# Splitting a gate/up stage into two token halves, and where a layer norm and the down weights then stand

## What is computed

```python
x = x + _layernorm(_L0_attn_ref(_layernorm(x), W_spin, b_spin, W_global, W_J, beta))
x = x + _layernorm(_L0_ffn_ref(_layernorm(x), w_gate, w_up, w_down))

# _L0_ffn_ref: D = 1024, H = 3072, int32 weights scaled by 1/127
gate = einsum('bsd,hd->bsh', x, wg); up = einsum('bsd,hd->bsh', x, wu)
h = silu(gate) * up
return einsum('bsh,dh->bsd', h, wd)
```

## Time and profile before

| | us |
|---|---|
| median of 2 runs (1460.48 to 1469.74) | 1465.11 |
| the profiled execution, slowest core | 1465.29 |
| its span in the trace (core 2) | 1463.7 |
| spans of the eight cores | 1441.8 to 1463.7 |
| PE busy in the span | 1208.2 (83%) |
| DVE, ACT, POOL busy | 494.7, 222.4, 72.9 |

### The profile page before, as it was taken

One profiled execution on the slowest core, in us unless ns is written; L12 is line 12 of the kernel. 1 busy time (PEld: TensorE's weight loads), 2 busy tenths in 40 slices (PEclk: granted clock), 3 DMA queues, 4 the chain that ended last, 5 costly groups with the idle time before them and its releaser, 6 DMA issues.

```text
span 1463.7 us, 14919 instructions; the slowest of 8 cores (1441.8 to 1463.7 us)
## 1 busy us (share of the span) xinstructions
PE 1208.2 (83%) x5274; PEld 517.7 (35%) x5274; DVE 494.7 (34%) x860; ACT 222.4 (15%) x359; POOL 72.9 (5%) x92
## 2 busy tenths in 40 slices
PE   0888887788989999999889810179999999999997
PEld 0233332233433434334333300034444444444443
DVE  2243334113434333333334246822122121134343
ACT  0111111211221111112211110021111111100000
POOL 0011110000000000000000000010110111000000
PEclk9999998989999999999989965589999999999999
DMA  9755557461232222122321179963463737323332
GB/s 191 144 138 131 133 131 179 98 101 28 52 65 44 51 44 43 44 51 44 62 52 38 36 151 242 298 100 36 45 75 40 86 32 84 30 62 111 98 104 86
DMA packets 230393, 131.04 MB, mean 90 GB/s; under 512 B 204720, under 2 KB 204720, under 8 KB 230320
## 3 DMA queue, kind: packets, MB, share of 16 engines
q10 hardware_dynamic: 156672, 50.35, 17.2%
q0 software_dynamic: 57744, 29.37, 15.5%
q1 hardware_dynamic: 15904, 50.37, 12.2%
HBM read 92.31 MB, written 25.17 MB: 80 GB/s over the span
## 4 chain that ended last, share of the span: by engine, by line
PE 62%; DVE 11%; DMA 11%; ACT 6%; ACTq 5%; issue 3%; DVEq 0%; SPq 0%
PE ps_pv L710 17%; PE ps_d L1136 11%; PE ps_u L1043 11%; PE ps_g L1032 11%; DMA xnT_sb<-xn_bf 6%; PE ps_s L256 6%; ACT P_sb L592 4%; ACTq L612 4%; DMA x_sc<-x_buf 3%; PE ps_e L305 2%; DVE tmp L728 1%; DVE qm L567 1%; DVE tmp L733 1%; ACT attn_wb L746 1%; PE ps_q L548 1%
## 5 line engine op out<-in xcount | busy, mean ns | idle before, releaser
L710 PE MATMUL ps_pv<-s_tok,PT_sb 128*128 128x512 bf16 x1024 | 249.1, 409 | 52.0 <-DVE PT_sb L673 51.1
L1032 PE MATMUL ps_g<-xn2T,wg_sb 128*128 128x512 bf16 x768 | 176.1, 388 | 100.7 <-DMA xn2T<-xn_bf 100.7
L548 PE MATMUL ps_q<-s_FM,ebuf 128*128 128x512 bf16 x1024 | 226.7, 382 | 7.6 <-DMA ebuf<-e_sc 7.6
L710 PEld LDWEIGHTS ps_pv<-s_tok,PT_sb 128*128 128x128 bf16 x1024 | 105.1, 104 | 195.9 <-issue 93.7
L1043 PE MATMUL ps_u<-xn2T,wu_sb 128*128 128x512 bf16 x768 | 169.7, 379 | 0.0
L1136 PE MATMUL ps_d<-wdT_sb,h_act 128*128 128x512 bf16 x768 | 165.9, 379 | 1.0 <-DVE h_act L1066 1.0
L1066 DVE SCALAR_TENSOR_TENSOR h_act<-silu_b,ps_u 128x512 bf16<-128x512 f32 x96 | 66.0, 688 | 266.5 <-PE ps_u L1043 265.4
L548 PEld LDWEIGHTS ps_q<-s_FM,ebuf 128*128 128x128 bf16 x1024 | 100.5, 98 | 131.1 <-issue 12.7
L1032 PEld LDWEIGHTS ps_g<-xn2T,wg_sb 128*128 128x128 bf16 x768 | 76.2, 100 | 196.7 <-issue 109.9
L256 PE MATMUL ps_s<-wspT_sb,xnT_sb 128*128 128x512 bf16 x512 | 137.6, 417 | 0.0
L1136 PEld LDWEIGHTS ps_d<-wdT_sb,h_act 128*128 128x128 bf16 x768 | 75.1, 98 | 91.9 <-issue 1.5
(11 more groups left out here) (74 smaller groups left out, 496.9 us busy)
## 6 DMA issues: line engine op xcount, KB each, us to landing
xs<-x SPq DMA_DIRECT2D x24, 1024.0 KB, 7.0
x_sc<-x_buf ACTq DMA_DIRECT2D x16, 512.0 KB, 6.7
xs<-x_sc SPq DMA_DIRECT2D x16, 512.0 KB, 4.3
out<-out_b SPq DMA_DIRECT2D x16, 512.0 KB, 5.1
wg_sb<-wgT POOLq DMA_DIRECT2D x24, 256.0 KB, 4.6
wu_sb<-wuT POOLq DMA_DIRECT2D x24, 256.0 KB, 5.4
wdT_sb<-wdT POOLq DMA_DIRECT2D x4, 1536.0 KB, 16.6
e_sc<-e_stage POOLq DMA_DIRECT2D x32, 128.0 KB, 2.4
```

Source lines behind the costliest of these rows:

```text
L548: i = t.matmul(ps_q[:, slot, half * 512:(half + 1) * 512], ebuf[:, qt % 2, j, :], s_FM[:, j, qi * 1024 + half * 512: qi * 1024 + (half + 1 ...
L710: i = t.matmul(ps_pv2[:, nb * 512:(nb + 1) * 512], PT_sb[:, par, cb * P:(cb + 1) * P], s_tok[:, cb, nb * 512:(nb + 1) * 512], start=(cb == ...
L1032: i = t.matmul(ps_g[:, tb, :], wg_sb[:, par, j, :], xn2T[:, j, tb * 512:(tb + 1) * 512], start=(j == 0), stop=(j == KC - 1))
```

## The change

1. **Token halves.** The FFN runs in two phases: phase 0 over `tb` 0 and 1, phase 1 over `tb` 2 and 3, each over all 24 blocks. A step (`ci`, 0 to 47) is one block in one phase and has 32 matmuls: gate of two `tb`, up of two `tb`. The same gate and up weights are loaded in each phase, so there are 48 pairs of loads where there were 24. The load for step ci+2 waits for the up matmuls of step ci.
2. **L2 in two pieces.** Slots 0 to 8 stay ahead of the FFN. Slots 9 to 15 are emitted one behind each of steps 0 to 6, and slot 16 behind step 7, on the same engines' streams.
3. **Down weights.** All four parts are emitted behind the whole FFN, and each waits for the part before it.
4. **Down matmuls.** A tile's 48 matmuls run in four segments of six hidden blocks, with the two output halves taken in turn; in tile 0 segment k waits for part k of the down weights.

The diff, cut to its core:

```diff
-        for t_i in range(NT_OWN + 1):
+        def l2slot(t_i):
             if t_i < NT_OWN:
                 l2_grpA(t_i)
             if t_i >= 1:
                 l2_grpB(t_i - 1)
-        s_flush()
+        for t_i in range(9):
+            l2slot(t_i)
...
-        def ffn_wload(hb):
-            sem = dwP[hb % 2]
-            w_war = rec.get(("up_mm", hb - 2, 3), 0)
+        def ffn_wload(ci):
+            hb = ci % HC
+            sem = dwP[ci % 2]
+            w_war = rec.get(("up_ci", ci - 2), 0)
...
         def wdT_part(i4):
-            def f(gp, i4=i4):
+            def f(gp, i4=i4, w_self=dwF.n):
+                gp.wait_ge(dwF.h, w_self)
...
-        ffn_wload(0)
-        ffn_wload(1)
-        wdT_part(0)
-
-        for hb in range(HC):
-            par = hb % 2
-            for tb in range(4):
+        def ffn_hb(ph, hb, tbs):
+            ci = ph * HC + hb
+            par = ci % 2
+            for tb in tbs:
...
-                    if hb >= 1:
-                        t.wait_ge(ss.h, rec[("silu", hb - 1, tb)])
+                    if wsl:
+                        t.wait_ge(ss.h, wsl)
...
+        ffn_wload(0)
+        ffn_wload(1)
+        for ph, tbs in ((0, (0, 1)), (1, (2, 3))):
+            for hb in range(HC):
+                ci = ph * HC + hb
+                ffn_hb(ph, hb, tbs)
+                if ci + 2 < 2 * HC:
+                    ffn_wload(ci + 2)
+                if ph == 0 and hb < 7:
+                    l2slot(9 + hb)
+                if ph == 0 and hb == 7:
+                    l2slot(16)
...
-            if hb == 6:
-                wdT_part(1)
-            if hb == 12:
-                wdT_part(2)
-            if hb == 18:
-                wdT_part(3)
...
+        for _i4 in range(4):
+            wdT_part(_i4)
...
-                    t.wait_ge(dwF.h, 64)
...
-                for nb in range(2):
-                    for cb in range(HC):
+                for seg in range(4):
+                    if t_i == 0:
+                        t.wait_ge(dwF.h, 16 * (seg + 1))
+                    for cb in range(seg * 6, (seg + 1) * 6):
+                        for nb in range(2):
```

More of the change, by code:

```diff
@@ L967, in build_program, with f @@
         wdT_r = wdT_d.rearrange("(c p) d -> p c d", p=P)
-        def ffn_wload(hb):
-            sem = dwP[hb % 2]
-            par = hb % 2
-            w_war = rec.get(("up_mm", hb - 2, 3), 0)
-            first = (hb <= 1)
-            def f(gp, hb=hb, sem=sem, par=par, w_war=w_war, first=first):
+        last_silu = {}
+        last_hmul_u = {}
+        last_silu_buf = {}
+        l2_done = {}
+        def ffn_wload(ci):
+            hb = ci % HC
+            sem = dwP[ci % 2]
+            w_war = rec.get(("up_ci", ci - 2), 0)
+            first = (ci <= 1)
+            def f(gp, hb=hb, sem=sem, par=ci % 2, w_war=w_war, first=first):
                 if first:
@@ L995, in ffn_wload @@
             sem.n += 32
-            rec[("wload", hb)] = (sem, sem.n)
+            rec[("wload_ci", ci)] = (sem, sem.n)
         def wdT_part(i4):
-            def f(gp, i4=i4):
+            def f(gp, i4=i4, w_self=dwF.n):
+                gp.wait_ge(dwF.h, w_self)
                 if i4 == 0:
@@ L1013, in wdT_part, with ftg @@
             dwF.n += 16
-        ffn_wload(0)
-        ffn_wload(1)
-        wdT_part(0)
-        for hb in range(HC):
-            par = hb % 2
-            for tb in range(4):
[L1022 to L1025, removed]
+        def ffn_hb(ph, hb, tbs):
+            ci = ph * HC + hb
+            par = ci % 2
+            for tb in tbs:
+                def ftg(t, hb=hb, par=par, tb=tb, first=(tb == tbs[0]),
+                        w4=rec[("xtr4", tb)], wl=rec[("wload_ci", ci)],
+                        wsl=last_silu.get(tb, 0)):
+                    if first:
+                        t.wait_ge(wl[0].h, wl[1])
                     if hb == 0:
@@ L1036, in build_program, with ftu @@
                 block.tensor(ftg)
[L1037 to L1041, removed]
+                rec[("g_ci", ci, tb)] = st.n
+            for tb in tbs:
+                def ftu(t, hb=hb, par=par, tb=tb,
+                        wuh=last_hmul_u.get(tb, 0)):
+                    if wuh:
+                        t.wait_ge(sv.h, wuh)
                     for j in range(KC):
@@ L1047, in build_program, with fsl @@
                 block.tensor(ftu)
[L1048 to L1053, removed]
+                rec[("u_ci", ci, tb)] = st.n
+            rec[("up_ci", ci)] = st.n
+            for tb in tbs:
+                def fsl(s, ci=ci, tb=tb, wt=rec[("g_ci", ci, tb)],
+                        prev=last_silu_buf.get(tb % 2, 0)):
                     s.wait_ge(st.h, wt)
@@ L1060, in build_program, with fvh @@
                 ss.n += 1
[L1061 to L1065, removed]
+                rec[("silu_ci", ci, tb)] = ss.n
+                last_silu[tb] = ss.n
+                def fvh(v, hb=hb, tb=tb, ci=ci,
+                        wsl=rec[("silu_ci", ci, tb)],
+                        wut=rec[("u_ci", ci, tb)]):
+                    v.wait_ge(ss.h, wsl)
+                    v.wait_ge(st.h, wut)
                     i = v.scalar_tensor_tensor(
@@ L1071, in build_program @@
                 block.vector(fvh)
-                rec[("hmul", hb, tb)] = sv.n
-            if hb + 2 < HC:
-                ffn_wload(hb + 2)
-            if hb == 6:
-                wdT_part(1)
-            if hb == 12:
-                wdT_part(2)
-            if hb == 18:
-                wdT_part(3)
[L1082 to L1085, removed]
+                rec[("hmul_ci", ci, tb)] = sv.n
+                last_hmul_u[tb] = sv.n
+                last_silu_buf[tb % 2] = sv.n
+        ffn_wload(0)
[10 more added lines that the diff above has]
+                    l2slot(16)
+                    l2_done.update(
+                        sv=rec[("xn2", NT_OWN - 1)],
+                        ss=rec[("sq3", NT_OWN - 1)],
+                        dt0=dtm[0].n, dt1=dtm[1].n,
+                        da0=da[0].n, da1=da[1].n,
+                        tr=[(s_, s_.n) for s_ in (dtp[0], dtp[1])])
+        hmul_done = rec[("hmul_ci", 2 * HC - 1, 3)]
+        ffn_done = dict(st=rec[("up_ci", 2 * HC - 1)],
+                        ss=rec[("silu_ci", 2 * HC - 1, 3)], sv=hmul_done)
+        ctx2.close()
         ctx23.close()
         ctxPS.close()
+        wdT_sb = ctx34.enter_context(
+            nc.sbuf_tensor("wdT_sb", [P, HC, D], BF16, side="right"))
+        for _i4 in range(4):
+            wdT_part(_i4)
         ctx4 = ExitStack()
@@ L1130, in ftd @@
                     t.wait_ge(sv.h, hmul_done)
-                    t.wait_ge(dwF.h, 64)
                 if t_i >= 2:
                     t.wait_ge(sv.h, rec[("d_evac", t_i - 2)])
-                for nb in range(2):
-                    for cb in range(HC):
[L1136 to L1139, removed]
+                for seg in range(4):
[3 more added lines that the diff above has]
+                        for nb in range(2):
+                            i = t.matmul(ps_d[:, par, nb * 512:(nb + 1) * 512],
+                                         h_act[:, cb, t_i * P:(t_i + 1) * P],
+                                         wdT_sb[:, cb, nb * 512:(nb + 1) * 512],
+                                         start=(cb == 0), stop=(cb == HC - 1))
                 vinc(st, i)
```

## The result

| | us |
|---|---|
| before, median | 1469.44 |
| changed, median of 11 runs | 1511.27 |
| changed, second comparison, median of 4 runs | 1499.67 |
| ratio | 1.030, 95% interval 1.026 to 1.034 |
| second comparison of the same two kernels | 1.026, 1.021 to 1.030 |

The change costs 3%: by the two ratios 38 and 44 us of some 1465.

The account below looks back on a forecast made before the run. PE's FFN pace, the first down tile and a fixed 164.6 us were taken to set the end. The 1463.7 span plus 18.3 (later FFN end) plus 36.5 (late down weights) gave 1518.5, so 1520 us, range 1498 to 1545.

Parts of the forecast that it names:

- What bounds: Whole run: PE's FFN pace, 6.91 us for 32 matmuls, then the first down tile and a fixed rest set the end.
- E: End of the FFN's last up matmuls: 1287.39 before, forecast 1305.7, 18.3 us later.
- 164.6 us fixed: Behind the first down tile: 15 more tiles take 155.4 us and the rest of the span 9.2, unchanged.
- Start of the FFN: After slots 0 to 8: step 0 runs gate from 925.7, up ends at 932.6, DVE reaches slot 9 at 933.5.
- The ring: Slots 9 to 16: in-order ACT and DVE wait for each other, 11.5 us a turn, seven turns; PE idles 4.6 each.
- transpose issue from 6.2: Within a turn, on ACT: the transpose is issued 6.2 us after its start, behind a 1.28 table load and 0.39 root.
- The pace: Last 39 FFN steps: 7.3 us a step against 6.91 of PE, since a weight load of 7.7 has one step to hide.
- The down weights: Behind the FFN: four parts land one after another, first down tile at E + 48.2, not E + 11.7; 36.5 us more.
- 12.0 alone: Each down part after part 0, with no other load beside it, lands 12.0 us after issue, the profiled minimum.
- The ring does not bind: Rival, slots 9 to 16: ACT runs ahead, a turn is 7.3 us or less, time 1490; chance 0.10.
- Loads bind harder: Rival, FFN steps: each up landing takes 9.0, a step costs 8.8 us, time 1575; chance 0.08.
- A drain for each table load: Rival, ACT in slots 9 to 16: 1.38 us more per switch, seven turns 19 us longer, time 1539; chance 0.10.

Follow-up runs that it names:

- E6: Changed kernel with Identity in place of Silu, so no table loads (output not the reference's); profiled execution 1496.82 us, no ratio.
- e4: Changed kernel with three buffers of gate and up weights in place of two; 1493.27 us, ratio 1.020.
- e12: Changed kernel with three weight buffers and the four down parts early under the FFN, ACT's order left as changed; 1469.19 us, ratio 1.004.
- e5: Changed kernel with four early down parts, three weight buffers, and ACT's slot work behind the next step's Silus; 1446.95 us, ratio 0.987.
- e10: Changed kernel with L2 whole ahead of the FFN and down parts early as before, so token halves stay; 1513.79 us, ratio 1.031.
- e2: Changed kernel with the four down parts issued behind steps 9, 16, 23 and 30, not behind the FFN; 1499.17 us, ratio 1.028.
- e3: Changed kernel with ACT's second layer norm work of a slot placed behind the next step's two Silus; 1492.84 us, ratio 1.021.

## Why the prediction was right, and where its terms were off

The time, 1511, lies in the range (1498 to 1545) and on the side that was forecast, and the mechanism of each term was found. The sum itself is 22 us too high against the profile; that the first comparison's median lies only 9 under it is luck in part. By its own steps:

- **What bounds.** Right: PE's pace, E, the first down tile, and 164.6 us fixed (155.4 + 9.1 measured).
- **Start of the FFN**: slot 9 at 77.3 us after L2's start; measured 66 to 71. The gap between slots 8 and 9 is right (19.2 forecast, 18.9 on core 4). Slot 8 itself was read from core 2, where it came 58.1 after L2's start; on the eight cores before it is 47 to 59, mean 52.9. I took a chance value of the slowest core for a constant. 8 us.
- **The ring**: there, with its waits and its two table loads. A turn was forecast at 11.5 and is 10.3. The step that was off is "transpose issue from 6.2": it is issued at 5.1 in the turn above, for the issue does not wait for the table load or the root. Together with the last steps of the stretch that is 9 us by step 9. E6 shows that the loads of tables matter less than their sum: 4 to 6 us without them, not 18.
- **The pace**: 7.3 forecast; 7.30 on the slowest core, 7.19 mean, and e4 shows that late loads are the cause.
- **The down weights**: 36.5 forecast, 33.6 measured on the mean, 31.2 on core 4. There the parts were used at E + 14.5, 25.8 and 37.8, for a forecast of 17.4, 30.2 and 43.0. The clock was right (0.50 under the start of the last segment). Part 0 was issued at E - 16.6 and not at E - 12.0, because the last FFN step itself had to wait for weights (10.7 us behind the start of the one before); on the mean it is E - 13.7. The total spacing was right by two errors that cancel: the parts landed after 15.1, 15.3, 10.8 and 11.5 us, for 16.6 and three times 12.0, so "12.0 alone" does not hold for part 1 on any core (13.7 to 15.3). 5 us in all.
- **E and the time.** E was forecast 17 us too late, by the 8 and 9 above; so L2's gain was given back to within a microsecond, where I had it 18 in the red. With the 5 of the down weights the sum is 22 over core 4's span (1495.8 for 1518.5). The medians stand 9 and 20 under 1520. What puts 12 us between the two comparisons is not shown; the stages ahead of L2 alone end anywhere from 840 to 856 us on the eight cores of this profile.
- **Rivals.** The ring does not bind (0.10): turns of 10.3 in the changed kernel, and e12 against e5, show that it does. Loads bind harder (0.08): not in the changed kernel, but in e10 and e2, 7.75 and 7.93. A drain for each table load (0.10): no. In the turn above the load to Silu starts 0.14 us behind the transpose issue, Silu starts right behind the load, and turns are shorter than without a drain by my sum. There the load comes 1.2 us behind the root, which could hide a drain; with ACT's order changed it follows directly behind a Silu. In e5, core 1, it starts 0.01 us behind the end of two Silus, and the root 0.02 us behind the load (rows below). Where the Trainium skill ("ScalarE: Activation LUTs", What ACT_TABLE_LOAD costs) has 1380 ns more for each switch, these rows have no room for it; the 1283 ns of the load agree.
- **Not foreseen**: that the three costs cover each other. Undoing one gave 0 to 8 us where its own term was 15 to 36, because the next wait took its place: early down parts made weight loads late (e2), and ACT's order met late loads (e3).

The rows for the drain, e5, core 1, timeline of ACT:

```profile
942.56 1.09 ACT L1074 ACTIVATE silu_b<-ps_g 128x512 f32<-128x512 f32 x2
...
943.66 1.28 ACT L911 ACT_TABLE_LOAD   x1
...
944.96 0.39 ACT L911 ACTIVATE sqv<-mvb,c_b,c_sc 128x1 f32<-128x1 f32 x1
```

What stays open: why the first comparison shows some 10 us more loss than the profiles; why slots 0 to 8 take 49 us on the changed kernel and 53 before, on the mean (the work and the order are the same, the scatter is as large as the difference); and whether the delay of slot 9 with more buffers is from bandwidth or from the queues. None was tried.

## What to carry to other kernels

Cutting a loop step in half doubles the loads of what is reused and halves the time that each has to hide in: check the step against issue plus landing (here 7.1 against 6.9), not only against bandwidth, and give it a third buffer. When work of one stage is emitted between steps of another, follow the order on *every* engine once around: a helper engine that must finish the old stage before it serves the new one makes a ring even when no engine is full. And when one repair gives nothing, look in the trace for the wait that took its place before calling the theory wrong; here three repairs worth nothing, 6 and 8 us alone were worth over 50 together.

## What the runs showed that I had not expected

- A DMA issue on ACT overlaps a table load and an activation that stand ahead of it: transpose issued at 941.42 during a load from 940.75 to 942.03 and a root that ends at 942.44.
- A down part of 1.5 MB in the same POOL queue costs some 7 us and not its whole 12 to 15: in e10 one step of 10 to 12 and one of 8 to 9. It can slow the pair ahead of it too. On e2's core 1 the up load issued 0.9 us before the part landed after 9.6 us (5.4 for the one before that), the part itself after 18.6, and the pair behind it after 13.3 and 15.2. So part and pairs share the transfers; on the median of e2's 32 parts the up load ahead lands after 6.0 us and the one behind after 9.6.
- With one more pair of weight loads (0.5 MB written) at the start of L2 slot 9 comes 3 to 7 us later, with a second one 2 more. That the pair is the cause is argued, not shown.
